# First scores of a windowed attention: whole queries as weights, masked keys moving, masked blocks filled by GpSimd's DMAs

## The reference, cut to what matters

```python
q = (x @ wq.T + bq).reshape(B, S, H, D); k = ...; v = ...        # H = 16, D = 16
qw = q.reshape(B, nW, W, H, D); kw = k.reshape(B, nW, W, H, D)    # 16 windows of W = 128 in each batch
loc = jnp.einsum('bnihd,bnjhd->bnihj', qw, kw) * scale            # scores inside the own window
scores = zeros(B, S, H, S); own windows = loc; global tokens (64) += gq . gk * scale
attn = softmax(scores, axis=-1)                                   # outside the window: score 0, not masked
out = einsum('bihj,bjhd->bihd', attn, v).reshape(B, S, HID) @ wo.T + bo
x = layernorm(x + out); x = layernorm(x + experts(x))
```

## Time and profile before

| | us |
|---|---|
| median of 3 runs | 444.06 |
| lowest, highest | 442.19, 445.27 |
| span of the profiled execution, first to last instruction | 442.8 |
| steps 4 to 27 (six turns of the loop) | about 33.4 a turn of four windows |
| PE, DVE, ACT, POOL busy | 405.3, 326.1, 250.6, 220.4 |

### The profile page before, as it was taken

The page is one execution under the profiler, slowest core; times in us unless marked ns, Lnnn a source line. Parts: engine busy times, 40 slices in busy tenths (PEclk is TensorE's granted clock), DMA queues, the critical chain, the costliest instruction groups (busy, mean ns, idle before and its releaser), DMA issues.

```text
span 442.8 us, 14658 instructions
## 1 busy us (share of the span) xinstructions
PE 405.3 (92%) x5747; PEld 339.8 (77%) x5747; DVE 326.1 (74%) x796; ACT 250.6 (57%) x523; POOL 220.4 (50%) x301
## 2 busy tenths in 40 slices
PE   5899799999999999999999899988798998999991
PEld 4758678888888888888888778756577887777891
DVE  6785687758757757757759888563668998899785
ACT  3424665675575575575576576676663555544421
POOL 4361343464464464464464566435733485477540
PEclk9999999999999999999999999999989999999997
DMA  8663740000000000000020000000000011011004
GB/s 240 186 199 111 240 137 4 27 25 0 24 24 0 24 24 0 24 24 0 24 72 4 25 2 3 3 1 2 0 2 2 1 49 47 0 47 49 34 15 143
DMA packets 21720, 20.34 MB, mean 46 GB/s; under 512 B 3133, under 2 KB 21682, under 8 KB 21682
## 3 DMA queue, kind: packets, MB, share of 16 engines
q1 hardware_dynamic: 16900, 15.07, 10.9%
q10 hardware_dynamic: 4782, 4.75, 3.3%
HBM read 15.41 MB, written 4.41 MB: 45 GB/s over the span
## 4 chain that ended last, share of the span: by engine, by line
PE 52%; DVE 26%; ACT 9%; issue 8%; DMA 3%; ACTq 1%; DVEq 0%; POOL 0%; POOLq 0%
DVE row_max_t L1154 10%; PE ps L1461 7%; PE ps L1737 7%; PE ps L1424 7%; PE ps L1562 5%; PE ps L1384 5%; PE ps L1415 4%; PE ps L1438 3%; PE ps L1444 3%; ACT probs L847 3%; DVE k_part L1013 2%; ACT boundsT_t L858 2%; PE ps L1406 2%; DMA rows<-in_L_attn_x_dram 2%; ACT k_part L713 2%
## 5 line engine op out<-in xcount | busy, mean ns | idle before, releaser
L847 ACT ACTIVATE probs<-ps 128x1024 f32<-128x1024 f32 x64 | 62.1, 1022 | 68.2 <-PE ps L1428 68.2
L1154 DVE TENSOR_REDUCE row_max_t<-ps 128x16 f32<-128x2048 f32 x31 | 70.9, 2287 | 3.7 <-PE ps L1415 3.6
L1737 PE MATMUL ps<-w_part,hm_part 128*128 128x256 f32 x384 | 53.8, 289 | 1.8 <-DVE hm_part L1332 1.8
L1415 PE MATMUL ps<-k_part,q_part 32*128 32x128 f32 x1584 | 51.5, 274 | 3.1 <-issue 1.5
L1415 PEld LDWEIGHTS ps<-k_part,q_part 32*128 32x128 f32 x1584 | 46.9, 186 | 9.2 <-issue 7.0
L1562 PE MATMUL ps<-xh_parts,w_part 128*128 128x512 f32 x192 | 53.8, 416 | 0.0
L557 POOL TENSOR_TENSOR q_part<-qf,q_part 128x512 fp32r<-128x512 f32 x32 | 41.0, 1281 | 25.7 <-ACT q_part L695 25.7
L599 POOL TENSOR_TENSOR attn_t<-num_t,rden_t 128x256 f32<-128x256 f32 x32 | 20.0, 624 | 64.7 <-DVE rden_t L1185 64.7
L1737 PEld LDWEIGHTS ps<-w_part,hm_part 128*128 128x128 f32 x384 | 48.2, 190 | 4.8 <-DVE hm_part L1332 2.4
L788 ACT ACTIVATE ffn_rows<-ps,b1s 128x512 f32<-128x512 f32 x32 | 22.0, 687 | 42.2 <-PE ps L1562 34.1
L1562 PEld LDWEIGHTS ps<-xh_parts,w_part 128*128 128x128 f32 x192 | 34.7, 194 | 6.5 <-issue 0.6
(11 more groups left out here) (234 smaller groups left out, 906.4 us busy)
## 6 DMA issues: line engine op xcount, KB each, us to landing
table<-rest_sums SPq DMA_DIRECT2D x4, 1088.0 KB, 6.1
xs<-in_L_attn_x_dram SPq DMA_DIRECT2D x16, 256.0 KB, 2.8
rows<-in_L_attn_x_dram ACTq DMA_DIRECT2D x4, 1024.0 KB, 8.1
out_dram<-yout SPq DMA_DIRECT2D x6, 512.0 KB, 2.9
w<-in_L_ffn_W_dram SPq DMA_DIRECT2D x2, 256.0 KB, 7.6
w<-in_L_ffn_W_dram SPq DMA_DIRECT2D x1, 512.0 KB, 4.2
out_dram<-yout SPq DMA_DIRECT2D x2, 256.0 KB, 2.6
out_dram<-yout ACTq DMA_DIRECT2D x2, 256.0 KB, 2.8
```

The lines of the kernel that those rows point to most:

```text
L847: act.activation(probs[:, 2 * h:2 * h + 2, :], ps[:, 2 * h:2 * h + 2, :], ACT.Exp).then_inc(probs_ready, 1)
L1154: dve.tensor_reduce(row_max[:], ps_all, op=ALU.max, axis=AX.X).then_inc(max_ready, 1)
L1415: last = mm(ps[:, u, (2 * c + a) * P:(2 * c + a + 1) * P], q_part[x][quad(u), s, c, a, :], k_part[y][quad(u), s, c, :], start=(i == 0), st ...
L1737: mm(y, hm_part[a][:, 1 - p, f, c * P:(c + 1) * P], w2_part[b][:, f, :], start=(f == 0 and i == 0), stop=False)
```

## The change

The masks move from the queries' product to copies. Queries and keys are both kept whole (`q_part`, `k_part`: split in high and low by ACT and DVE in two instructions each, for two windows; POOL's subtraction and DVE's four masked instructions go). The masked blocks `q_apart` and `k_apart` are zeroed once, and for each pair of windows POOL starts four DMAs, SBUF to SBUF, of 64 partitions x 2 x 512 numbers (256 KB): two copy the even and the odd partitions of the keys, two those of the queries. For that the numbers of the two heads of a quadrant are interleaved on even and odd partitions, by the order in which the weights and biases are laid out. The first scores then are 24 products with whole queries as weights and masked keys moving (256 columns); the turned ones keep their number and take their moving side from `q_apart`. The scores of the global tokens and of windows 0 and 1 stay at 48 products. Each masked block exists once, so its DMA waits until the last product that reads the old one is done. `k_apart` lies in the experts' `xh_parts`, which is why `take_high(0, 0)` moves from step 30 to step 31, and is zeroed by POOL in the run of constants.

```diff
@@ GpSimd @@
-            def q_low(w, s):
-                need(pool, turned_scores_in_psum, w - 3)
-                pool.wait_ge(q_high_ready, w // 2 + 1)
-                pool.tensor_tensor(q_part[1][:, s], qf[:, s % 2], q_part[0][:, s].bitcast(fp32), ALU.subtract).then_inc(q_ready, 1)
+            def part_keys(s):
+                for a in range(2):
+                    pool.dma_start(k_apart[a:P:2, :, a], k_part[a:P:2, :, s // 2]).then_inc(k_apart_ready, 16)
+            def part_queries(s):
+                for a in range(2):
+                    pool.dma_start(q_apart[a:P:2, :, a], q_part[a:P:2, :, s // 2]).then_inc(q_apart_ready, 16)
...
+                if live(t + 1, steady) and p:
+                    pool.wait_ge(k_ready, t // 2 + 2)
+                    pool.wait_ge(scores_in_psum, t + 1)
                 if pp:
...
-                if live(t + 1, steady) and (steady or t > 0):
-                    q_low(t + 1, (s + 1) % SLOTS)
+                if live(t + 1, steady) and p:
+                    part_keys((s + 1) % SLOTS)
...
+                    if p == 0 and (steady or t > 0):
+                        pool.wait_ge(q_ready, t // 2 + 1)
+                        pool.wait_ge(turned_scores_in_psum, t)
                     pool.tensor_tensor(e_arg[:, p, :], table[:, bass.ds(t * EXW + NV, HEADS)], guard[:, p, :],
                                        ALU.subtract).then_inc(e_arg_ready, 1)
+                    if p == 0 and (steady or t > 0):
+                        part_queries(s)
...
+            pool.wait_ge(wT_in_psum, 4)
+            pool.tensor_tensor(xh_parts[:, 0].rearrange("p i c n -> p (i c n)"), zeros16[:, 0:1].broadcast_to([P, 4 * GT]), ...).then_inc(k_apart_zero, 1)
             pool.memset(ident_b[:], 0.0).then_inc(late_const, 1)
@@ ScalarE @@
             def queries_of(w, s):
-                copy(q_part[0][:, s:s + 2], qf[:]).then_inc(q_high_ready, 1)
+                need(act, turned_scores_in_psum, w - 3)
+                act.wait_ge(q_in_psum, w // 2 + 1)
+                for c in range(KC):
+                    last = act.activation(q_part[:, 0, s // 2, c]..., ps_xq[:, c * 2 * P:(c + 1) * 2 * P], ACT.Identity, bias=bq_scaled[:, c:c + 1])
@@ VectorE @@
+            def queries_of(w, s):
+                dve.wait_ge(q_high_ready, w // 2 + 1)
+                for c in range(KC):
+                    last = dve.scalar_tensor_tensor(q_part[:, 1, s // 2, c]..., ps_xq[:, c * 2 * P:(c + 1) * 2 * P], bq_scaled[:, c:c + 1], q_part[:, 0, s // 2, c]..., ALU.add, ALU.subtract)
@@ TensorE @@
+            def scores(s):
+                for c in range(KC):
+                    for i, (x, y) in enumerate(SPLIT):
+                        for u in range(UNITS):
+                            last = mm(both(c, u), q_part[quad(u), x, s // 2, c, s % 2, :], k_apart[quad(u), y, :, c, s % 2, :],
+                                      start=(i == 0), stop=(i == 2), tile_position=(32 * u, 0))
```

More of the change, by code:

```diff
@@ L756, in _ @@
             keys_of(0, 0)
-            queries_of(0, 0)
+            act.wait_ge(q_ready, 1)
+            copy(q_apart[:, 0].rearrange("p a c w n -> p (a c w n)"), qf.rearrange("p a c w n -> p (a c w n)")).then_inc(q_high_ready, 1)
             load_rows(2)
@@ L842, in step @@
                     keep_onehot(0, 0)
+                if ahead and p == 0:
+                    queries_of(t + AHEAD, (s + AHEAD) % SLOTS)
                 if prev:
@@ L1034, in _ @@
             dve.wait_ge(qg_ready, 1)
[L1035 removed]
+            first_queries()
             keys_of(0, 0)
@@ L1576, in step @@
                     need(pe, probs_ready, 2 * (t - 1))
-                    pe.wait_ge(q_ready, t + 1)
-                    pe.wait_ge(k_ready, t // 2 + 1)
-                    scores(s).then_inc(scores_in_psum, 1)
+                    if not steady and t == 1:
+                        pe.wait_ge(first_low_ready, 2)
+                        pe.wait_ge(k_ready, 1)
+                        scores_by_queries(q_apart[:, :, :, :, 1, :], k_part[:, :, 0, :, 1, :]).then_inc(scores_in_psum, 1)
+                    else:
+                        pe.wait_ge(q_ready, t // 2 + 1)
+                        if p == 0:
+                            pe.wait_ge(k_apart_ready, 2 * 16 * (t // 2))
+                        scores(s).then_inc(scores_in_psum, 1)
                 if pp:
@@ L1708, in _ @@
             pe.wait_ge(gs_scaled, B)
-            pe.wait_ge(q_ready, 1)
-            scores(0).then_inc(scores_in_psum, 1)
+            pe.wait_ge(first_low_ready, 1)
+            pe.wait_ge(k_ready, 1)
+            scores_by_queries(q_apart[:, :, :, :, 0, :], k_part[:, :, 0, :, 0, :]).then_inc(scores_in_psum, 1)
             pe.wait_ge(consts_ready, 1)
```

139 lines of the change are left out of this document (86 added, 53 removed).

## The result

The changed kernel takes **454.87 us** (median of 4 runs, 452.31 to 455.61) where the kernel before takes 444.66 beside it (4 runs): a ratio of 1.0229 with a 95% interval of 1.0185 to 1.0274. It is 10 us slower; I had forecast 439.3 and a range up to 452. The profiled execution has a span of 453.4 us against 442.8, at a mean granted clock of 0.969 against 0.989.

The account below looks back on a forecast made before the run. Bound: chains to DVE's row maximum, with TensorE's queue close behind. Gains of 4.8 (loop) and 2.2 (0.8 + 0.4 + 1.0) less 2.2 for zeroing gave 4.8 us less, 444.06 to 439.3; range 435 to 452.

Parts of the forecast that it names:

- six turns x 0.8: Loop: each turn of four windows gains 0.75 to 0.8 us, counted for six turns as 4.8 us.
- The loop: A turn goes from 33.4 to 32.6 us, with TensorE waiting for the row maximum in even steps.
- The price of 24 products: First scores on TensorE: 24 products of 256 columns take 0.86 us, where 48 narrow ones took 1.56.
- GpSimd's DMAs: GpSimd's queue: each DMA issue taken as 1.0 us, landing 2.8 us after; keys have 0.8 us to spare, queries 2.3.
- I cost the DMAs at nothing: GpSimd's four DMAs per pair of windows: issues up to 1.3 us each are free, so their price is 0.
- a gain of 0.4 more: Steps 24 to 26, where DVE sets the pace: shorter work on the queries gains 0.4 us.
- The zeroing: Start: GpSimd's zeroing of k_apart takes 4.4 us, makes the first bounds late and TensorE wait, +2.2 us.
- ScalarE's high part: Queries' high part on ACT takes 0.84 us, in idle time before the exponentials: no price in the loop.
- Start and tail: Start costs 0; step 31 gains 0.7 us from an earlier maximum and loses about as much by copies before the routing: 0.
- A: Rival, chance 0.24: DMAs come late or block GpSimd, slower; 449 us at 1.5 us per issue, about 475 at 2.
- d: What one DMA start costs GpSimd's queue: unknown, bounds 0 and 2.2 us, taken as 1.0.
- The rule of the Trainium skill: GpSimd's DMAs: it can't write descriptors during VectorE's fast-mode copies, 3.1 us for a transfer instead of 0.62; noted against the change.

Follow-up runs that it names:

- e8: Changed kernel, but from step 24 on SyncE instead of GpSimd issues the DMAs that fill q_apart and k_apart; 451.37 us, ratio 1.0177.
- e10: Changed kernel with first scores from window 2 on as 48 products of 128 columns instead of 24 of 256; 457.00 us, ratio 1.0326.
- e1: Changed kernel with GpSimd's zeroing of k_apart moved from behind its part of the dg subtraction to the head of its step 1; 449.18 us, ratio 1.0124.
- e7: Changed kernel with the zeroing kept in its place but done as GpSimd's memset instead of a multiplication; 449.50 us in a single run.
- b1: Kernel before with only GpSimd's zeroing added and the two early tiles swapped in the layout; 448.03 us, ratio 1.0102.
- e2: Changed kernel with ScalarE, in step 0 alone, making the queries' high part behind the global scores' exponentials and x_rest; 453.22 us, ratio 1.0205.
- e3: Changed kernel with VectorE's two take_high(0, 0) copies moved from ahead of step 31's routing to behind its moments' copy; 450.89 us, ratio 1.0152.
- b2: Kernel before with only the two take_high(0, 0) copies moved from the end of step 30 to ahead of step 31's routing; 446.89 us, ratio 1.0073.

## Why the prediction was wrong, point by point

- **The sum's turns**: "six turns x 0.8" counts steps 24 to 27 as a turn of the loop, which they are not by `LOOP_A`. I read no rows of them, and there lay one of the losses. Once it is gone the 0.8 is there (e8: 34.00 for 34.79). Two smaller slips: 1.56 less 0.86 is 0.70 and not 0.63, and the zeroing would have been hidden under 2.5 us, not 2.7 (34.79 - 0.22 - 32.05). Neither moves the forecast.
- **The loop** was right: 32.6 a turn forecast, 32.40 measured; TensorE waits for the row maximum in both kinds of step, no wait for k_apart or q_apart in it. The price of 24 products was 0.86 by the earlier trace rows and is 0.98. e10 shows the wide products to be the source, as the sum had it, with 0.93 a turn for 0.8.
- **GpSimd's DMAs** were sized right (1.0 taken, 0.63 measured; landing 2.8 and 2.6) and free in the loop. The failed step is "I cost the DMAs at nothing", carried over to steps 24 to 28, where I had counted a gain of 0.4 more. I had looked only at what waits for a landing or for `attn_t`; that VectorE's SBUF instructions beside GpSimd's next ones are held I had not priced. Without the issues (e8) these steps take 34.00 instead of 39.51: 2.6 us of it by the holding, 2.9 by the clock's falls, which e1 and e7 don't have.
- **The zeroing**: the step that failed is "the first bounds come at 36.45 + 0.22 = 36.7", for which TensorE was to wait, and the +2.2 taken from it. The zeroing took 3.59 us, not 4.4, and the bounds held nobody. It made VectorE's dg subtraction 3.0 us longer (4.26 for 1.22), and so held TensorE, which then ran at half clock. e1 and b1 price it at about 4 us at step 1.
- **ScalarE's high part**: "ACT's 0.84 lies in its idle time ... No price in the loop" is right for the loop, but step 0 has the exponentials of the global scores behind it, which I never placed in the new order. e2 prices it at 3.6 us at step 1, all of which the table's loads took back.
- **Start and tail**: "the copies then delay the routing by about as much: 0" failed. I had costed two copies of 0.43 against a wait of 0.7, and left out that they take 1.57 beside GpSimd's `rows`, GpSimd's `take_low`, which they release beside the routing, and the clock. e3 and b2 price it at 5.1 and 3.5 us in the tail.
- **The rivals**: A named the right side, by a mechanism (late landings, d above 1.4) that didn't decide; only its clause on the table's loads came true, as 1.1 us in after and up to 5.2 once the start was repaired. The rule of the Trainium skill that I quoted (SBUF — State Buffer, the "DVE blocks DMA" trap: VectorE's copies in a fast mode keep GpSimd from writing descriptors) was hardly tried: of VectorE's copies from SBUF to SBUF only one of 24 x 256 (0.27 us, at 61.14) lay beside a GpSimd issue in after, and those two issues took 1.26 us, as elsewhere. What showed is the other direction, GpSimd keeping VectorE out, for which the prediction has no term.

## What to carry to other kernels

When a change gives GpSimd a long instruction or a DMA, list what VectorE does from SBUF to SBUF beside it in every stage, the peeled steps too, and ask who waits for that: a steady loop whose VectorE reads PSUM says nothing about them. A new instruction in one engine's queue is costed in the first and last steps as well, with everything that it is put ahead of and everything that it releases. A stall of 2 to 3 us on TensorE here cost 1 to 3 us more by the clock (e1: 4.1 us for a wait of 2.96; e3: 5.1 for 2.12), though not always: after waits of 1.8 us in step 26 the clock was 0.57 in after and 1.00 in e1. And a stage that starts earlier meets other traffic, so repairs are measured together.
